# High butterfly stages of a decoder layer as matrix products, in 66 pieces among the recurrence's steps

## The reference, cut

```python
x = x + ssm(layernorm(x))        # linear recurrence; its scan runs over the 4 batches
x = x + xattn(layernorm(x), ctx) # 16 heads, context of 77 tokens
x = x + ffn(layernorm(x))

# ffn: 512 -> 2048 -> 512, two butterflies of 11 stages each
h = einsum('bsd,dh->bsh', x, W_exp) + b_exp
h = butterfly(h, up_weights, 2048)
h = gelu(h + up_bias)
h = butterfly(h, down_weights, 2048)
y = einsum('bsh,hd->bsd', h, W_con) + b_con + down_bias

# butterfly, stage s pairs index i with i + 2**s:
a, b = y[..., nb, 0, s], y[..., nb, 1, s]
na, nb2 = w00 * a + w01 * b, w10 * a + w11 * b
```

## Time and profile before

| | us |
|---|---|
| median of 3 runs | 2364.82 |
| lowest, highest | 2364.71, 2370.11 |
| the profiled execution | 2366.6 |
| its span, first to last instruction | 2364.8 |

### The profile page before, as it was taken

One profiled execution on the slowest core, in us unless ns is written; L12 is line 12 of the kernel. 1 busy time (PEld: TensorE's weight loads), 2 busy tenths in 40 slices (PEclk: granted clock), 3 DMA queues, 4 the chain that ended last, 5 costly groups with the idle time before them and its releaser, 6 DMA issues.

```text
span 2364.8 us, 42243 instructions
## 1 busy us (share of the span) xinstructions
PE 2226.1 (94%) x15752; PEld 1943.3 (82%) x15752; DVE 1769.8 (75%) x2969; ACT 1293.1 (55%) x2832; POOL 557.2 (24%) x619
## 2 busy tenths in 40 slices
PE   8877789999999999969999999999999999999998
PEld 4777668778777877748998998988989989989898
DVE  5999668878878887755875867857858758678567
ACT  2998556666667666543644635535536446355343
POOL 3788222222222322200030030020210300300203
PEclk9888879999999999989999999999999999999999
DMA  8555702332332232256568677676685686776765
GB/s 329 192 178 189 263 2 77 116 124 77 108 116 94 85 119 90 95 182 219 172 219 267 199 218 227 208 262 179 212 263 177 214 266 200 223 221 210 225 188 177
DMA packets 190883, 424.47 MB, mean 179 GB/s; under 512 B 27342, under 2 KB 64718, under 8 KB 190286
## 3 DMA queue, kind: packets, MB, share of 16 engines
q1 hardware_dynamic: 190696, 421.94, 55.1%
HBM read 331.29 MB, written 90.60 MB: 178 GB/s over the span
## 4 chain that ended last, share of the span: by engine, by line
PE 65%; DVE 16%; ACT 11%; issue 4%; DMA 3%; POOL 1%; SPq 0%; DVEq 0%; ACTq 0%; POOLq 0%
PE ps L416 52%; PE ps L1805 5%; ACT es L982 5%; PE ps L1773 2%; DVE gl L1178 2%; DVE G L1530 2%; DVE st L1149 2%; DVE ptl L1178 1%; DVE wc_s L1178 1%; PE ps L1784 1%; DMA xa<-in_x 1%; DVE rsum L1401 1%; ACT wc_h L939 1%; DVE rmax L1390 1%; ACT pth L957 1%
## 5 line engine op out<-in xcount | busy, mean ns | idle before, releaser
L416 PE MATMUL ps<-ring,gh 128*128 128x256 f32 x3584 | 654.4, 285 | 12.6 <-DVE gl L1178 12.5
L416 PEld LDWEIGHTS ps<-ring,gh 128*128 128x128 f32 x3584 | 558.0, 192 | 16.9 <-DVE gl L1178 15.7
L416 PE MATMUL ps<-xth,ring 128*128 128x512 f32 x1792 | 554.6, 390 | 4.2 <-ACT U L1066 4.2
L416 PE MATMUL ps<-ring,gl 128*128 128x256 f32 x1792 | 506.8, 283 | 0.0
L416 PEld LDWEIGHTS ps<-xth,ring 128*128 128x128 f32 x1792 | 337.4, 188 | 74.7 <-issue 4.6
L1054 ACT ACTIVATE gh<-G 128x512 fp32r<-128x512 f32 x384 | 237.2, 629 | 212.4 <-PE ps L416 212.1
L416 PE MATMUL ps<-xtl,ring 128*128 128x512 f32 x896 | 349.5, 390 | 0.0
L416 PEld LDWEIGHTS ps<-ring,gl 128*128 128x128 f32 x1792 | 343.4, 192 | 0.0
L1178 DVE TENSOR_TENSOR gl<-G,gh 128x512 fp32r<-128x512 f32 x384 | 278.8, 739 | 57.2 <-ACT gh L1054 55.6
L759 POOL TENSOR_TENSOR es<-es,rinv 128x308 f32<-128x308 f32 x256 | 180.2, 735 | 456.5 <-DVE rinv L1405 456.5
L1470 DVE TENSOR_TENSOR U<-ps,U 128x512 f32<-128x512 f32 (+1 forms) x168 | 137.3, 817 | 169.5 <-PE ps L416 166.9
(11 more groups left out here) (212 smaller groups left out, 4646.0 us busy)
## 6 DMA issues: line engine op xcount, KB each, us to landing
ring<-wup_scratch SPq DMA_DIRECT2D x224, 512.0 KB, 3.8
ring<-wdn_scratch SPq DMA_DIRECT2D x224, 512.0 KB, 3.6
X<-x_scratch SPq DMA_DIRECT2D x32, 1024.0 KB, 8.5
xa<-in_x SPq DMA_DIRECT2D x16, 1024.0 KB, 5.5
x_scratch<-xa SPq DMA_DIRECT2D x16, 1024.0 KB, 4.3
x<-x_scratch SPq DMA_DIRECT2D x16, 1024.0 KB, 5.6
x_scratch<-x SPq DMA_DIRECT2D x16, 1024.0 KB, 4.3
out_x<-X SPq DMA_DIRECT2D x16, 1024.0 KB, 6.3
```

The source lines that it names most:

```text
L416: mm = pe.matmul(bank, a, b, start=first and i == 0, stop=last and i == n - 1, skip_group_check=go_on)
```

## The change

The elementwise high stages leave all steps. Instead the four high stages of each butterfly become, for each place within the chunks, a matrix over the 16 chunks:

- VectorE builds in the set-up, from the stage weights loaded once per partition (`hw`, 1 MB each, 512-byte runs), the products along each path (`pick_bit`, `join`), 16 x 16 per partition; GpSimd spreads them into block matrices `mq` (128 partitions = 16 chunks x 8 places).
- A row group is brought to that layout by SBUF to SBUF transfers. Up: the low-stage product of a chunk (piece LU) is copied by ScalarE to one of eight stage buffers and sent by SP to eight neighbouring partitions of `xg`; the high product (UH) then reads `xg` and goes to `wu_d`. Down: `yg` is loaded in the regrouped layout, the high product (DH) goes through a stage buffer to eight partitions of `yd`, 16 apart; then the low product (DL) goes to `wd_d`.
- BL and BH are the same for the bias, which is regrouped through DRAM with 4-byte runs. That makes 16 + 1 + 16 + 1 + 16 + 16 = 66 pieces, handed out over the 16 steps by `PER_GROUP` and ahead of each of a step's four feature blocks by `pieces_at`. Piece UH 0 waits until all LU transfers have landed, DH 0 until `yg` has, DL 0 until all DH transfers have.
- `xa` gets five slots instead of four, each with a semaphore; SP no longer waits for a store before the next transfer it issues. The recurrence's four result banks become two; the pieces use two banks.
- The query products of the first attention block move into and behind the last step; the part between recurrence and attention is gone. Other tiles move in SBUF.

The diff, cut to its core:

```diff
+        LU, BL, UH, BH, DH, DL = 0, MC, MC + 1, 2 * MC + 1, 2 * MC + 2, 3 * MC + 2
+        PIECES = 4 * MC + 2
+        PER_GROUP = [6, 6, 5, 0, 4, 4, 4, 5, 4, 4, 4, 4, 0, 5, 5, 6]
+        assert sum(PER_GROUP) == PIECES and len(PER_GROUP) == NG
+        staged = lambda n: n - (n > BL) - (n > BH)
...
+        def pieces_at(g, c):
+            first, m = group_end(g) - PER_GROUP[g], PER_GROUP[g]
+            return range(first + (m * c + 3) // KC, first + (m * c + m + 3) // KC)
...
+            sp.dma_start(ident[:, :], ident_in).then_inc(ident_loaded, 16)
             sp.dma_start(cT[:, :, :], ctxT).then_inc(kctx_loaded, 16)
             sp.dma_start(wk[:, :, :], rows(wkT)).then_inc(kctx_loaded, 16)
+            by_row = lambda w: w.rearrange("q s k e -> q (s k e)").unsqueeze(0).broadcast_to([MC, P, HIS * (MC // 2) * 4])
+            sp.dma_start(hw[0][:, :, :, :, :, :], by_row(hi_up)).then_inc(hw_loaded[0], 16)
+            sp.dma_start(hw[1][:, :, :, :, :, :], by_row(hi_dn)).then_inc(hw_loaded[1], 16)
             sp.dma_start(wv[:, :, :], rows(wvT)).then_inc(wv_loaded, 16)
             sp.dma_start(wgu[:, :], lo_up).then_inc(lo_loaded[0], 16)
...
+            sp.dma_start(ubg[:, :], upbias.rearrange("(l j) c -> c l j", j=MC), allow_slow_non_contiguous=True).then_inc(bias_loaded, 16)
...
             sp.dma_start(wgd[:, :], lo_dn).then_inc(lo_loaded[1], 16)
-            sp.wait_ge(kt_stored, 32)
-            load_x(1)
-            load_yd(0)
+            sp.wait_ge(path_ready, 2)
+            load_x(2)
...
+            def piece_out(n):
+                sp.wait_ge(piece_act, n + 1)
...
+                if n == BH:
+                    return
+                src, out = stage[staged(n) % STAGES][:, :], stage_out[staged(n) % STAGES]
+                if n < BL:
+                    c = n - LU
+                    sp.dma_start(xg[c * LG:(c + 1) * LG, :, :], src).then_inc(out, 16)
+                elif n < BH:
+                    sp.dma_start(wu_d[n - UH], src).then_inc(out, 16)
+                elif n < DL:
+                    sp.dma_start(yd[n - DH:P:MC, :, :], src).then_inc(out, 16)
+                else:
+                    to = wd_d.rearrange("j (c l) n -> c l j n", c=MC)
+                    sp.dma_start(to[n - DL], src).then_inc(out, 16)
+
+            for g in range(NG):
+                for c in range(KC):
+                    for n in pieces_at(g, c):
+                        piece_out(n)
+                    if c == 1:
+                        if g:
+                            stored(sp, x1_stored, g - 1)
+                        if g and g + 4 < NG:
+                            load_x(g + 4)
+                        n = g - (NG - 3)
+                        if n in (0, 1):
+                            after(sp, x1_loaded, n * 16)
+                            sp.dma_start(x1[:, n, :, :], x1_ld[n]).then_inc(x1_loaded, 16)
+                    if (g, c) == (3, 0):
+                        sp.wait_ge(piece_pe, BL)
+                        sp.dma_start(yg[:, :, :], wcon.rearrange("(p j) n -> p j n", j=MC)).then_inc(yg_loaded, 16)
...
+                sp.wait_ge(x1_ready, KC * g + KC)
+                sp.dma_start(x1_st[g], xa[:, xslot(g), :, :]).then_inc(x1_stored, 16)
...
+            low_paths(wgd, False, lo_loaded[1], tdn_ready)
             rsqrt(1, xn1_ready, T)
...
+            for g in range(NG - 1):
+                rsqrt(g + 2, xn1_ready, T * (g + 2))
+                if g < 2:
+                    high_matrix(g)
...
+            def piece_back(n):
+                act.wait_ge(piece_pe, n + 1)
+                bank = ps[:, 6 + n % 2, :]
+                if n in (BL, BH):
+                    ins = A(blo[:, :] if n == BL else up_b[:, :], bank[:, 0:MC], ACT.Copy)
+                else:
+                    after(act, stage_out[staged(n) % STAGES], stage_turns(n))
+                    ins = A(stage[staged(n) % STAGES][:, :], bank, ACT.Copy)
+                ins.then_inc(piece_act, 1)
...
+            act.wait_ge(tup_ready, 1)
+            act.wait_ge(tdn_ready, 1)
+            for g in range(NG):
+                for c in range(KC):
+                    for d in {0: (0, 1), 1: (2, 3)}.get(c, ()):
+                        if g + 1 < NG:
+                            hi1_piece(g + 1, d)
+                    if c > 1 and g + 2 < NG:
+                        apply1(g + 2, range(2 * c - 4, 2 * c - 2))
...
+                    for n in pieces_at(g, c):
+                        piece_back(n)
...
+            def pick(out, first, second, b):
+                picks(V.tensor_scalar(out, first, bits[:, b, 0:1], None, ALU.mult))
+                return V.scalar_tensor_tensor(out, second, bits[:, b, 1:2], out, ALU.mult, ALU.add)
...
+            bit_masks()
+            for i in range(HIS):
+                pick_bit(0, i)
+            join(0)
...
+                if k == 0:
+                    pick_bit(1, 0)
                 if k == 1:
                     stats1(0)
+                if k == 2:
+                    for i in range(1, HIS):
+                        pick_bit(1, i)
+                    join(1)
             for k in range(NB):
                 dve.wait_ge(r_hi, k + 1)
...
+            for g in range(NG):
+                lows = [lambda c=c: lo1_piece(g + 1, c) for c in range(KC)] if g + 1 < NG else []
+                if g + 2 < NG:
+                    stats1(g + 2, [lows[0], lows[1], None, None])
+                    lows = lows[2:]
...
+                    n = KC * g + c
+                    dve.wait_ge(s5_done, n + 1)
+                    xs = xa[:, xslot(g), :, c * P:(c + 1) * P].rearrange("p t (b n) -> p b t n", b=2)
+                    V.tensor_tensor(xs, xs, ps[:, 4 + n % 2, :].rearrange("p (b t n) -> p b t n", b=2, t=T), ALU.add).then_inc(x1_ready, 1)
+                    if c == 0:
+                        for low in lows:
+                            low()
...
+            def out1(g, c):
+                n = KC * g + c
+                after(pe, x1_ready, max(n - 1, 0))
+                pe.wait_ge(lo1_done, n + 1)
+                for b in range(2):
+                    for h in range(2):
+                        at = (2 * b + h) * P
+                        sl, w = slice(at, at + P), (NB - 2 * h) * HS
+                        out_at = (b + 1) * NB * HS
+                        mm = split3(pe, ps[:, 4 + n % 2, out_at - w:out_at],
+                                    [(xt1h[:, g % 2, c, sl], xt1l[:, g % 2, c, sl], rh[:, 0:w], rl[:, 0:w])],
+                                    first=(h == 0), last=(h == 1))
+                mm.then_inc(s5_done, 1)
...
+            def piece(n):
+                after(pe, piece_act, max(n - 1, 0))
+                bank = ps[:, 6 + n % 2, :]
...
+                elif n < BH:
+                    j = n - UH
+                    if j == 0:
+                        pe.wait_ge(mq_ready, 1)
+                        for out in stage_out:
+                            pe.wait_ge(out, stage_turns(UH))
+                    for k in range(KC):
+                        cols = slice(k * P, (k + 1) * P)
+                        mm = pe.matmul(bank[:, cols], xg[:, j, cols], mq[0][:, j, :], start=True, stop=True)
...
+                elif n < DL:
+                    j = n - DH
+                    if j == 0:
+                        pe.wait_ge(mq_ready, 2)
+                        pe.wait_ge(yg_loaded, 16)
+                    mm = pe.matmul(bank, mq[1][:, j, :], yg[:, j, :], start=True, stop=True)
...
+            pe.wait_ge(ident_loaded, 16)
+            pe.wait_ge(r_lo, NB)
+            t1(0)
+            pe.wait_ge(kv_lo, KC + NB)
+            for g in range(NG):
+                if g + 1 < NG:
+                    t1(g + 1)
+                else:
+                    pe.wait_ge(xn2_ready, 1)
+                    pe.wait_ge(lo1_done, KC * NG)
+                    for k in range(KC):
+                        turn2(ps[:, k, :], k).then_inc(pre_pe, 1)
+                for c in range(KC):
+                    for n in pieces_at(g, c):
+                        piece(n)
+                    out1(g, c)
+                    if g == NG - 1 and c > 1:
+                        pe.wait_ge(wq_lo, 1)
+                        pe.wait_ge(pre_lo, KC)
+                        query(ps[:, c - 2, :], c - 2).then_inc(pre_pe, 1)
+            for o in range(2, KC):
+                query(ps[:, o, :], o).then_inc(pre_pe, 1)
+            pe.wait_ge(x1_ready, KC * NG)
+            pe.wait_ge(piece_act, PIECES)
 
             def turn3(p, i, bank):
                 pe.wait_ge(xn3_ready, 2 * p + 2)
```

More of the change, by code:

```diff
@@ L571, in load_wc @@
             def load_wc(n):
-                for j in range(4):
-                    sp.wait_ge(fold_stored[j], 16 * 2)
+                for out in stage_out:
+                    sp.wait_ge(out, stage_turns(PIECES))
                 after(sp, wc_stored, 32 * n)
@@ L1015, in attn_act @@
                 if isinstance(g, int) and g == 0:
-                    for j in range(4):
```

(54 more changed lines are left out.)

515 lines of the change are left out of this document (172 added, 343 removed).

## The result

The changed kernel takes 2428.88 us (median of 4 runs, 2427.0 to 2432.97) against 2364.77 us; the ratio is 1.0264, 95% interval 1.0246 to 1.0281. It is slower by 64 us. The forecast was 2401 with a range up to 2426: right in its sign and in its mechanism for the up weights, too small by 28 us, since it counted nothing for the down weights. The profiled execution is the one of 2432.97 us, its span 2431.2.

A forecast was written before the change was run, and what follows sets the result against it. VectorE's butterfly work was taken to bound the steps. With it gone, scores would start at 276 us plus 42 waiting for up-weight transfers, 318 against 281.35: 2366.6 + 37 - 1.8, taken as 2401 us, range 2354 to 2426.

The forecast's parts named there:

- (f): Regrouping transfers: 5.4 us per up-weight piece, TensorE standing 42 us at step 4; down transfers nothing, 10 us in range.
- (d): Set-up: VectorE's path matrices 6.9 us twice; the queue ends last, wgd lands at 59.4 us, block 1 transposed at 73.9.
- (a): Steps: butterfly work leaves ScalarE, VectorE and GpSimd; VectorE keeps 8.9 us, a step without pieces takes 9.0.
- (b): Steps: 66 pieces enter TensorE, together 66 us; a low-stage piece 0.86 us, a UH piece 0.96.
- (c): Steps: TensorE bounds the heavy ones, such as 12.5 us for steps 0 and 1, 16.2 for step 7.
- (e): Sum with transfers hidden: scores start at 276 us against 281.35, including 4 us for short waits and lower clock.
- rival (2): Regrouping transfers hide, at up to 2.9 us a piece: 2359.4 us, within 2349 to 2368; chance 0.32.
- rival (3): Transfers hide, but set-up packets cost 81 ns each, wgd 17 us later: 2376 us; chance 0.08.
- What would show it: Signs: TensorE idle tens of us before first UH, low DMA rate at high share, scores near 318, rest 2083.5 us.

The follow-up runs named there:

- e1: Changed kernel with each up-weight (LU) regrouping transfer written into all 128 partitions, not eight neighbours, weights in the wrong order: 2386.2 us.
- e2: Changed kernel with both up and down regrouping transfers written into all 128 partitions, both regroupings thus left out: 2363.3 us.
- e3: Changed kernel with each up-weight transfer written into eight partitions 16 apart, not eight neighbours, weights in the wrong order: 2406.8 us.
- e13: Changed kernel with both transfers into all 128 partitions, and GpSimd normalising block 1 before multiplying out the second low-stage weights: 2358.6 us.

## Why the prediction was wrong

**The failed step is the sentence of (f) on the down weights: "I count nothing, and 10 us in the range".** By the medians the 64 us are 2428.9 - 2386.2 = 42.7 for the up transfers, 2386.2 - 2363.3 = 22.9 for the down transfers, and -1.5 for all the rest. The forecast had 42 for the first, nothing for the second, -5.4 for the rest. The reason given for nothing, four transfers to a step and a free step behind them, looked only at whether DL 0 would wait. It does (10.2 us), but more is lost before: from the first UH to the first DL product e1 takes 128.8 us and e2 100.3 (profiled executions). By an estimate from e3's 155 ns a packet, four transfers keep half of the engines busy for 4 x 128 x 155 ns/8 = 10 us of a step of 11, and each store and load of x needs those engines too. SP's issues of x towards the end of DH, in the kernel after:

```profile
253.01 0.45 SPq L553 DMA_DIRECT2D x_scratch<-xa  x1
...
269.97 0.38 SPq L475 DMA_DIRECT2D xa<-in_x  x1
...
271.68 0.77 SPq L553 DMA_DIRECT2D x_scratch<-xa  x1
...
284.75 0.38 SPq L475 DMA_DIRECT2D xa<-in_x  x1
```

The two stores take 17.0 and 13.1 us to land, and each holds the next load back. The premise of (d) that a block of x lands 5.3 us after its issue failed with it: over 62 to 353 us the median is 9.5 us for a load and 12.4 for a store.

**The range was too short at its upper end** for the same reason. It put "x blocks queued among them and DH slow too" at 24 us above the forecast (2425); the miss is 28, of which 22.9 are the down transfers and 3.9 a gain in the rest that came smaller than forecast.

**(f) for the up weights is right in its total, by errors that cancel.** I took 5.4 us a piece by halving a bound; it is 4.0. And I took the transfers as having the engines for themselves, but two stores and two loads of 1 MB stand among them, and the first piece was sent at 84.4 and not 75.4: 84.4 + 16 x 4.0 + 4 x 2.7 = 159, against 163.4 forecast and 165.9 measured; seven microseconds this sum doesn't name. The estimate by the Trainium skill (SBUF — State Buffer, the same section) in the prediction, 4.8 us and 2391 us, was nearer per piece and farther in the total, since it too left those out. That the 42 us came out as 42.7 is luck in this sense: the mechanism is shown, its sizes were not right one by one.

**(a), (b), (c), (e) hold.** With the regroupings out and the set-up near its forecast (e13: the first LU product at 75.1, forecast 73.9 for block 1) the steps up to the first UH product take 48.9 us (forecast 47.7), those up to the first DL product 101.9 (102.0); the scores start at 273.3 against 276, and the time is 2358.6 against the 2359.4 of rival (2). A UH piece took 1.06 us (e2, first row), where (b) said 0.96. So rival (2) was the right price of the change if its transfers hid, and it failed at its own condition: 4.0 us a piece where 2.9 decide. The 4 us that (e) adds for short waits and the lower clock are not enough once TensorE waits: 16.8 us, as shown under e2.

**(d) is wrong in its way and small in its effect.** wgd landed at 55.3, not 59.4, 12.8 us later than before where (d) had 17 and at least 15, and GpSimd began then; so rival (3), dear short packets, is out. But I had the queue as what ends last. It was VectorE: its path matrices took 7.7 us for the up weights (forecast 6.9) and, in two parts, 24 us for the down weights (30.7 to 41.6 and 51.7 to 64.8 us). Some 12 us of that are four instructions that stand beside GpSimd's products: 2.42, 4.61, 2.09 and 4.23 us where 0.3 to 0.5 is usual. The first transposes began at 67.1 and not at 47, block 1 was transposed by 82.8 and not at 73.9. That is worth 4.7 us (e2 to e13), where nothing else holds.

**What would show it:** TensorE's wait before the first UH product, ending with a DMA into xg, is there. This product comes 35.9 us later than in e2: 22.7 are that wait, 6.3 other idle time of TensorE in these steps, 3.4 the lower clock, and 3.5 a later start of the steps. The rate is low at a high share, and the rest kept its length. The first scores matmul near 318 was wrong: 350.8.

## What to carry to other kernels

Before a transfer into few partitions is put beside others, price it per engine, by how many partitions it writes and how near they lie, and then price what else those engines carry: narrow transfers that left the mean share at 52% here made a wide one five times as long to land, from either queue. A regrouping that is counted as hidden because nobody waits for its result can still cost through the loads and stores beside it; ask what their landing time becomes, and what TensorE's granted clock is among its waits. Two elementwise engines given work in the same stretch of the set-up may work one after the other; look at the duration of one instruction with and without the neighbour.

## What the runs showed of the hardware

- SBUF to SBUF, 256 KB in 2 KB packets (ns a packet as in the experiments): into 8 neighbouring partitions 66 to 74 GB/s on 8 engines (247 ns a packet); 8 partitions 16 apart 155 ns on 8 engines; 16 neighbours 115 GB/s on 16 engines (292 ns); 16 partitions 8 apart 114 ns; all 128 78 ns, about as in the stretch before of the earlier trace rows (81).
- A 1 MB store issued behind such transfers took 21.8 us from the same queue and 21.7 us from another, where 4.3 is usual.
- VectorE's 128x256 product of two SBUF tiles took 0.42 us alone and 4.23 us while GpSimd multiplied.
- The same some 1350 TensorE instructions took 210.6 us at a granted clock of 0.86, among waits, and 193.8 us at 0.97 (after, e2).
